# A gated recurrence of 2048 steps on one core: low fp16 parts by a scan, products in a staggered order, a hint on TensorE's outer loop

## The reference

```
z = sigmoid(y_t @ W_z + h @ U_z + vz)
r = sigmoid(y_t @ W_r + h @ U_r + vr)
hh = tanh(y_t @ W + (r * h) @ U + vh)
h = (1 - z) * h + z * hh          # out_t = y_t + h
```

## Time and profile before

| | us |
|---|---|
| median of 3 runs | 7111.71 (7102.33 to 7116.66) |
| the profiled execution | 7111.03 |
| its span, first to last instruction | 7109.2 |
| TensorE matmul busy | 6224.6 (88%) |
| VectorE busy | 5234.9 (74%), 43503 instructions |
| ScalarE busy | 3359.5 (47%) |
| mean granted TensorE clock | 0.971 |

### The profile page before, as it was taken

How to read it: one execution, slowest core, us unless ns; L and a number is a source line. 1 busy time by engine, 2 the same in 40 slices (tenths; PEclk the granted TensorE clock), 3 DMA queues, 4 the chain that set the end, 5 groups by cost and what they waited for, 6 DMA issues and landing times.

```text
span 7109.2 us, 488208 instructions
## 1 busy us (share of the span) xinstructions
PE 6224.6 (88%) x200232; PEld 5779.7 (81%) x200232; DVE 5234.9 (74%) x43503; ACT 3359.5 (47%) x22603; POOL 3.5 (0%) x13
## 2 busy tenths in 40 slices
PE   7888888888888888888888888888888888888888
PEld 7888888888888888888888888888888888888887
DVE  6777777777777777777777777777777777777777
ACT  3444444444444444444444444444444444444444
POOL 0000000000000000000000000000000000000000
PEclk8999999999999999999999999999999999999999
DMA  2000000000000000000000000000000000000000
GB/s 81 19 17 16 17 19 17 19 15 19 17 19 17 15 18 19 17 19 15 18 17 19 17 18 15 19 17 19 17 16 17 19 17 19 15 19 17 18 17 16
DMA packets 80595, 134.55 MB, mean 19 GB/s; under 512 B 12336, under 2 KB 18480, under 8 KB 80304
## 3 DMA queue, kind: packets, MB, share of 16 engines
q1 hardware_dynamic: 80304, 129.81, 5.3%
HBM read 20.46 MB, written 8.65 MB: 4 GB/s over the span
## 4 chain that ended last, share of the span: by engine, by line
PE 68%; DVE 26%; issue 5%; ACT 0%; SPq 0%; DMA 0%; ACTq 0%; DVEq 0%
PE pair_r L252 27%; PE ps_z L252 23%; PE pair_h L252 17%; DVE pair_h L481 8%; DVE h_part L528 4%; DVE h_part L518 4%; DVE h_part L537 4%; DVE keep L519 2%; DVE h_part L523 2%; DVE zn L532 2%; PE ps_p L224 0%; PE ps_z L212 0%; DMA u_raw<-in_L_cond_U 0%; DVE rh_part L490 0%; DVE ps_z L481 0%
## 5 line engine op out<-in xcount | busy, mean ns | idle before, releaser
L252 PEld LDWEIGHTS pair_r<-h_part,u_part 128*128 128x128 f16 x65536 | 1783.8, 96 | 1146.9 <-DVE h_part L537 1027.8
L252 PE MATMUL pair_r<-h_part,u_part 128*128 128x32 f16 x65536 | 1985.4, 177 | 801.9 <-DVE h_part L537 686.2
L252 PE MATMUL pair_h<-rh_part,u_part 128*128 128x32 f16 x65536 | 2120.3, 177 | 9.7 <-DVE rh_part L499 8.3
L252 PE MATMUL ps_z<-h_part,u_part 128*128 128x32 f16 x65536 | 1971.2, 177 | 45.4 <-issue 45.4
L252 PEld LDWEIGHTS pair_h<-rh_part,u_part 128*128 128x128 f16 x65536 | 1907.2, 96 | 104.4 <-DVE rh_part L499 11.6
L252 PEld LDWEIGHTS ps_z<-h_part,u_part 128*128 128x128 f16 x65536 | 1802.2, 96 | 48.0 <-issue 48.0
L481 DVE TENSOR_REDUCE pair_r<-pair_r 128x4 f32<-128x20 f32 x4096 | 742.4, 186 | 744.8 <-PE pair_r L252 723.4
L345 ACT ACTIVATE pair_r<-pair_r 128x4 f32<-128x4 f32 x4096 | 640.6, 158 | 1360.8 <-DVE pair_r L481 1291.5
L481 DVE TENSOR_REDUCE pair_h<-pair_h 128x4 f32<-128x12 f32 x4096 | 717.7, 175 | 697.7 <-PE pair_h L252 697.7
L345 ACT ACTIVATE th_z<-ps_z 128x8 f32<-128x8 f32 x2048 | 362.6, 177 | 1132.8 <-DVE ps_z L481 1132.8
L345 ACT ACTIVATE pair_h<-pair_h 128x4 f32<-128x4 f32 x4096 | 647.0, 158 | 393.4 <-DVE pair_h L481 393.0
(11 more groups left out here) (70 smaller groups left out, 3299.5 us busy)
## 6 DMA issues: line engine op xcount, KB each, us to landing
w_stage<-w_in SPq DMA_DIRECT2D x384, 256.0 KB, 2.3
x_tok<-in_x SPq DMA_DIRECT2D x68, 128.0 KB, 2.6
out_dram<-o_tok SPq DMA_DIRECT2D x66, 128.0 KB, 2.4
mlp_w<-in_L_cond_W SPq DMA_DIRECT2D x2, 1024.0 KB, 6.8
u_raw<-in_L_cond_U_r SPq DMA_DIRECT2D x1, 1024.0 KB, 5.6
u_raw<-in_L_cond_U_z SPq DMA_DIRECT2D x1, 1024.0 KB, 7.7
u_raw<-in_L_cond_U SPq DMA_DIRECT2D x1, 1024.0 KB, 10.4
w_in<-in_L_cond_W_r SPq DMA_DIRECT2D x4, 256.0 KB, 9.8
```

Of the source, the lines that this page charges most:

```text
L252: last = nc.tensor.matmul(bank[:, SLOT * m:SLOT * m + WIDE].rearrange("p (r n) -> p r n", n=n), u_part[:, g, part, k, gm * P:(gm + 1) * P] ...
```

## The change

Three things are changed.

1. Low parts. The tile `r_scan` holds for each value three columns: 0, the tanh, h_cur; `n_scan` holds 0, the tanh, z_mul. The fp16 tiles get three columns too: for the high part of r * h (-1, -1, high), of new (-1, 0, high). A scan over these triples, state = factor * state - term, gives after the third step of each value (1 + tanh) * h - high, or z_mul * tanh - high: the low part, which it writes as the third column of the low tile. So the full fp32 value of a half is no longer computed before the low part; `zn` for h_cur is computed at the end, once for both halves. ScalarE writes the tanh results to SBUF instead of PSUM and no longer waits for `zn1`. The matmuls' moving operand is now the third column of each triple.
2. Order. `staggered` writes r and h in the same order: with the first input half, both output chunks of half 0 and one of half 1 (12 matmuls); after the second wait, half 0 with the second input half (its `_mm` semaphore after 20 matmuls); then the rest of half 1. On VectorE, high(0), low(0), high(1), low(1) follow one another, and the sum of h's half 1 stands ahead of `new_high(0)`.
3. TensorE's outer loop is opened with `hint_back_edge=True`, which puts a prefetch hint for the loop's closing branch at the top of each turn.

```
-        h_cur = sb("h_cur", [P, S])
-        h_part = sb("h_part", [P, K, 2 * PARTS, B], F16)
-        rh_part = sb("rh_part", [P, K, PARTS, B], F16)
+        r_scan = sb("r_scan", [P, S, 3])
+        n_scan = sb("n_scan", [P, S, 3])
+        h_cur, z_mul = r_scan[:, :, 2], n_scan[:, :, 2]
+        h_part = sb("h_part", [P, 2 * PARTS, K, B, 3], F16)
+        rh_part = sb("rh_part", [P, PARTS, K, B, 3], F16)
...
-                moving = parts[:, k, :, :].rearrange("p a b -> p (a b)").unsqueeze(1).broadcast_to([P, WIDE // n, n])
+                moving = parts[:, :, k, :, 2].unsqueeze(1).broadcast_to([P, WIDE // n, n // B, B])
...
+            def staggered(banks, g, parts, src, name, t1):
+                def product(mh, m, kh):
+                    for k in range(kh * HC, (kh + 1) * HC):
+                        last = tile_product(banks[mh], m, g, mh * HC + m, k, parts, k == 0 and m == 0)
+                    return last
+                pe.wait_ge(s[src + "0"], t1)
+                for m in range(HC):
+                    product(0, m, 0)
+                product(1, 0, 0)
+                pe.wait_ge(s[src + "1"], t1)
+                for m in range(HC):
+                    last = product(0, m, 1)
+                last.then_inc(s[name + "0_mm"], 1)
+                for m in range(1, HC):
+                    product(1, m, 0)
+                for m in range(HC):
+                    last = product(1, m, 1)
+                last.then_inc(s[name + "1_mm"], 1)
...
-                    for kh in range(2):
-                        pe.wait_ge(s[f"hs{kh}"], t1)
-                        for mh in range(2):
-                            for m in range(HC):
-                                for k in range(kh * HC, (kh + 1) * HC):
-                                    last = tile_product(ps_r[mh], m, R, mh * HC + m, k, h_part, k == 0 and m == 0)
-                            if kh == 1:
-                                last.then_inc(s[f"r{mh}_mm"], 1)
+                    staggered(ps_r, R, h_part, "hs", "r", t1)
...
-                    for mh in range(2):
-                        for kh in range(2):
-                            if mh == 0:
-                                pe.wait_ge(s[f"rh{kh}"], t1)
...
+                    staggered(ps_h, H, rh_part, "rh", "h", t1)
...
-            with pe.Fori(0, NB) as n:
+            with nc.Fori(0, NB, engines=[mybir.EngineType.PE], hint_back_edge=True) as n:
...
-                        tanh(ps_r[hf][:, TANH:TANH + HS], ps_r[hf], R, HS, f"r{hf}_sum", t1, f"r{hf}_th")
+                        tanh(r_scan[:, half[hf], 1], ps_r[hf], R, HS, f"r{hf}_sum", t1, f"r{hf}_th")
...
-                    act.wait_ge(s["zn1"], t1)
                     seed(pair_h, H, nxt)
...
+                def low(part, hi, hf, factors, done):
+                    V.tensor_tensor_scan(triples(part[:, hi + 1, kc[hf]]), factors[:, half[hf]].rearrange("p s c -> p (s c)"),
+                                         triples(part[:, hi, kc[hf]]), 0.0, ALU.mult, ALU.subtract).then_inc(s[done], 1)
...
-                gated_high(0)
-                gated_full(0)
-                gated_high(1)
-                gated_low(0)
-                gated_full(1)
-                gated_low(1)
+                for hf in range(2):
+                    gated_high(hf)
+                    gated_low(hf)
...
                 def new_low(hf):
-                    dve.wait_ge(s[f"zn{hf}"], t1)
-                    V.tensor_tensor(h_part[:, kc[hf], NEW + 1, :], kb(zn[:, half[hf]]), h_part[:, kc[hf], NEW, :],
-                                    ALU.subtract).then_inc(s[f"hs{hf}"], 1)
-
-                new_high(0)
+                    dve.wait_ge(s[f"nhi{hf}"], t1)
+                    low(h_part, NEW, hf, n_scan, f"hs{hf}")
+
                 dve.wait_ge(s["h1_mm"], t1)
                 total(ps_h[1], H, HC, "h1_sum")
-                new_full(0)
+                new_high(0)
                 keep_low()
                 new_low(0)
                 new_high(1)
-                new_full(1)
                 new_low(1)
-                V.tensor_tensor(h_cur[:, :], keep[:, :], zn[:, :], ALU.add).then_inc(s["h_ok"], 1)
+                V.tensor_tensor(zn[:, :], z_mul, n_scan[:, :, 1], ALU.mult).then_inc(s["zn_ok"], 1)
+                dve.wait_ge(s["zn_ok"], t1)
+                V.tensor_tensor(h_cur, keep[:, :], zn[:, :], ALU.add).then_inc(s["h_ok"], 1)
```

More of the change, by code:

```diff
@@ L92, in gru_kernel @@
         keep = sb("keep", [P, S])
-        z_mul = sb("z_mul", [P, S])
         zn = sb("zn", [P, S])
@@ L113, in gru_kernel @@
                  "seed0 h0_ready r0_mm r1_mm z_mm z_keep h_ok h0_mm h1_mm r0_sum r1_sum z_sum h0_sum h1_sum r0_th r1_th z_th h0_th h1_th "
-                 "rh32_0 rh32_1 rh0 rh1 keep_ok zn0 zn1 hs0 hs1 copied")
+                 "rhi0 rhi1 rh0 rh1 keep_ok nhi0 nhi1 hs0 hs1 zn_ok copied scan_zero")
         s = {n: ctx.enter_context(nc.semaphore("s_" + n)) for n in names.split()}
@@ L249, in tile_product @@
                 n = (ADDENDS[g] - 1) * B
-                moving = parts[:, k, :, :].rearrange("p a b -> p (a b)").unsqueeze(1).broadcast_to([P, WIDE // n, n])
+                moving = parts[:, :, k, :, 2].unsqueeze(1).broadcast_to([P, WIDE // n, n // B, B])
                 for part in range(PARTS):
-                    last = nc.tensor.matmul(bank[:, SLOT * m:SLOT * m + WIDE].rearrange("p (r n) -> p r n", n=n),
+                    last = nc.tensor.matmul(bank[:, SLOT * m:SLOT * m + WIDE].rearrange("p (r a b) -> p r a b", a=n // B, b=B),
                                             u_part[:, g, part, k, gm * P:(gm + 1) * P], moving,
@@ L362, in steps @@
                     A(z_keep[:, :], th_z[:, :], ACT.Copy, scale=-0.5, bias=0.5).then_inc(s["z_keep"], 1)
-                    A(z_mul[:, :], th_z[:, :], ACT.Copy, scale=H_SCALE / 2, bias=H_SCALE / 2)
-                    tanh(ps_h[0][:, TANH:TANH + HS], ps_h[0], H, HS, "h0_sum", t1, "h0_th")
+                    A(z_mul, th_z[:, :], ACT.Copy, scale=H_SCALE / 2, bias=H_SCALE / 2)
+                    tanh(n_scan[:, half[0], 1], ps_h[0], H, HS, "h0_sum", t1, "h0_th")
                     seed(ps_z, Z, nxt)
-                    tanh(ps_h[1][:, TANH:TANH + HS], ps_h[1], H, HS, "h1_sum", t1, "h1_th")
-                    act.wait_ge(s["zn1"], t1)
+                    tanh(n_scan[:, half[1], 1], ps_h[1], H, HS, "h1_sum", t1, "h1_th")
                     seed(pair_h, H, nxt)
@@ L384, in _ @@
             act.wait_ge(s["h_ok"], T)
-            A(hist[:, (T - 1) % (2 * TB), :], h_cur[:, :], ACT.Copy).then_inc(s["copied"], 1)
+            A(hist[:, (T - 1) % (2 * TB), :], h_cur, ACT.Copy).then_inc(s["copied"], 1)
             put_out(NB + 1)
@@ L482, in total, with triples @@
                                        cols(bank, g, 0, m).rearrange("p m a b -> p m b a"), AX_X, ALU.add).then_inc(s[done], 1)
+            def triples(a):
+                return a.rearrange("p k b c -> p (k b c)")
             def step(t1):
                 kc = (slice(0, HC), slice(HC, K))
+                def low(part, hi, hf, factors, done):
+                    V.tensor_tensor_scan(triples(part[:, hi + 1, kc[hf]]), factors[:, half[hf]].rearrange("p s c -> p (s c)"),
+                                         triples(part[:, hi, kc[hf]]), 0.0, ALU.mult, ALU.subtract).then_inc(s[done], 1)
                 def gated_high(hf):
                     dve.wait_ge(s[f"r{hf}_th"], t1)
[L490 to L495, removed]
+                    V.scalar_tensor_tensor(rh_part[:, 0, kc[hf], :, 2], kb(r_scan[:, half[hf], 1]), 1.0,
+                                           kb(h_cur[:, half[hf]]), ALU.add, ALU.mult).then_inc(s[f"rhi{hf}"], 1)
                 def gated_low(hf):
-                    dve.wait_ge(s[f"rh32_{hf}"], t1)
-                    V.tensor_tensor(rh_part[:, kc[hf], 1, :], kb(rh[:, half[hf]]), rh_part[:, kc[hf], 0, :],
-                                    ALU.subtract).then_inc(s[f"rh{hf}"], 1)
+                    dve.wait_ge(s[f"rhi{hf}"], t1)
+                    low(rh_part, 0, hf, r_scan, f"rh{hf}")
                 for hf in range(2):
@@ L517, in step @@
                 dve.wait_ge(s["z_keep"], t1)
[L518 to L519 removed]
+                V.tensor_tensor(h_part[:, KEEP, :, :, 2], kb(z_keep[:, :]), kb(h_cur), ALU.mult)
+                V.tensor_tensor(keep[:, :], z_keep[:, :], h_cur, ALU.mult).then_inc(s["keep_ok"], 1)
                 def keep_low():
                     dve.wait_ge(s["keep_ok"], t1)
[L523 removed]
+                    V.tensor_tensor(h_part[:, KEEP + 1, :, :, 2], kb(keep[:, :]), h_part[:, KEEP, :, :, 2], ALU.subtract)
                 def new_high(hf):
                     dve.wait_ge(s[f"h{hf}_th"], t1)
[L528 to L533 removed]
+                    V.tensor_tensor(h_part[:, NEW, kc[hf], :, 2], kb(z_mul[:, half[hf]]),
+                                    kb(n_scan[:, half[hf], 1]), ALU.mult).then_inc(s[f"nhi{hf}"], 1)
                 def new_low(hf):
[L536 to L540 removed]
```

(3 more changed lines are left out.)

25 lines of the change are left out of this document (9 added, 16 removed).

## The result

| | before | changed |
|---|---|---|
| median, us | 7112.88 (7102.33 to 7116.66, 4 runs) | 8899.45 (8873.95 to 8921.37, 4 runs) |
| span of the profiled execution | 7109.2 | 8918.2 |
| mean granted TensorE clock | 0.971 | 0.514 |
| VectorE busy, instructions | 5234.9, 43503 | 5228.9, 37359 |

The changed kernel takes 1.2513 times as long as the one before, with a 95% interval of 1.2467 to 1.256. The forecast was 6715 us, 0.944 times. The page of the changed kernel has the granted clock, the instruction queue and the chain that ended last as follows; they answer to the earlier trace rows.

A forecast was written before the change was run, and what follows sets the result against it. One loop-carried chain through TensorE and VectorE was taken as the bound. 7111 less 287 (shorter step) less 113 (hint) is 6711, put at 6715 us for turns that gain less; own range 6640 to 6775, 8-in-10 range 6620 to 6940.

The forecast's parts named there:

- The moving operand: TensorE's matmuls read at a stride of three fp16 values: no cost taken; reading at half pace would cost 0.13 us a step.
- rival 1: Reads of k = 2 straddle 16-byte lines: 1.6 ns more for a quarter of the matmuls, 6785 us; chance 0.10.
- Rival 4: Strided read sets TensorE's pace, three columns' time spent for each: 40 ns a matmul, 9190 us; chance 0.08.
- The scan and the tail: On VectorE a scan takes 0.18 us; `new_high(0)` to `new_low(0)` falls from 0.34 to 0.195, gain 0.145.
- The stagger: TensorE's r and h order: both 0.07 us waits inside the step go; h's half 0 costs 0.10 on the chain.
- The hint: At TensorE's outer-loop turns the 3.15 us stop goes, 98 us, and 15 us of the second pause; together 113 us.
- a pause of about 1.0 stays: Second pause at an outer-loop turn, in TensorE's first step: about 1.0 us where 1.37 was; 15 us taken as gained.
- nine instruction blocks as before: Sign in the instruction queue: each outer-loop turn still fetches nine blocks, 288 in all before the change.

## Why the prediction was wrong

**The step that failed is "The moving operand"**: "I take nothing, the lower bound, and keep 0.13 and worse as rivals". The measured price is 0.97 us a step, 1994 of the 2184 us between forecast and measurement. The strided read alone in the kernel before gives 1.2576, the contiguous read in the changed kernel 0.973. The bound of 0.13 was wrong because I took the low clock's pace, 0.87 for 32 matmuls, for that of a read at half pace, and this for the worst of the likely cases. Chunk 2 is read at 60 / 32 = 1.9 ns a column, two and a quarter times the low clock's pace, at either clock.

The mechanism was named in rival 1, with its place (chunk 2, bytes 28 and 34) and the page of the Trainium skill that describes it (SBUF — State Buffer, the note on cachelines in the section Door 1: The DMA port swizzle); only its price, 1.6 ns a matmul, was an estimate from the wrong row. It is 34 ns for each of those matmuls and 6 for the other ones of r and z. The Trainium skill's rule, 16-byte lines that want two hits each, agrees with the 60 ns that moved with the straddling pair and left with it (of the width of a line the runs rule out 8 bytes, but not 32). It doesn't explain that r and z stay at 31 ns with two hits a line. An estimate from the rows comes nearer: a straddling operand changes its line at each of 32 columns, 60 / 32 = 1.9 ns a change, and one with two values a line at 16, which makes 30. But h changes its line 16 times too, between two lines and not four, and stays at 25; no run here settles why. Rival 4 had the size by luck: 40 ns a matmul against 38 measured on the average, 9190 us against 8899. Its mechanism, the time of three columns for each one read, would have made all chunks alike. Its chance of 0.08 was too small for an operand whose only evidence was cover that no row had tested.

**The clock**, of which the forecast said nothing for the changed kernel, fell to 0.514. It did not follow the pace of the matmuls alone: the means are 0.97 in the kernel before and 0.94, 0.912 and 0.909 in three others whose 32 matmuls of 32 columns take 0.82 us (contiguous read, the same in the old order, stagger alone), 0.907 where z takes 0.97, 0.51 at 1.22, and 0.50 with 8 or 16 columns. What lowers it stays open. It costs little by itself, 106 us where the columns were cut to 8 in the kernel before.

**The scan and the tail** were right: 183 ns, 0.19 from high to scan, a step of 3.21 to 3.23 against 3.205. Three things are missing in the 190 us between 6715 and the 6905 with contiguous reads. The store of the projection (90 us) was not in the sum, though h_cur moved back and r's sums forward. The wait for hs1 is 0.04, where I had 0.01, and the ordinary step 0.03 longer (57 us for 2048). And the step after the one without a projection takes 3.38, some 0.14 more, 54 us for 384 of them. The packed trace shows what stands in it: VectorE turns its inner loop there (branch at 3008.04, register work until 3008.47), between h_cur and r's first sum, which comes 0.93 after the step's start instead of 0.74; with the store left out it is the same 0.94. In the kernel before, whose h_cur is earlier, the sum comes at 0.80 in this step as in the others. No run takes the branch away. The 19 us that the hint gave beyond the forecast go against these: 90 + 57 + 54 - 19 = 182 of the 190.

**The stagger** was right in sum, as the ordinary step shows, but I had booked it in two places as if its gain were its own. By itself it loses 260 us; it gains only together with the scan.

**The hint** gained 132 us against 113. The step "a pause of about 1.0 stays" was wrong: both pauses went. So was the sign "nine instruction blocks as before": there are 8 or 9 in all instead of 288.

## What to carry to other kernels

When an edit changes how TensorE's moving operand lies in SBUF, look first at where the bytes of neighbouring columns lie against 16-byte boundaries; a layout made for one engine's instruction (here the scan's triples) is paid by every matmul that reads it. That a matmul takes some nanoseconds longer than its columns need is no bound for a read that no row shows: test it alone first. And when a chain is shortened, work that was hidden behind its slack, as the fifth step's store, has to be counted again.

## What the runs showed of the hardware

- A matmul of 32 fp16 moving columns, eight or four values repeated, at clock 1.00: 25 ns contiguous. As pairs in four places 48 or 64 bytes apart, the two of a pair 6 or 8 bytes apart and in one 16-byte line, 30 to 31; in two such places 25. With the pair on two sides of a boundary 60. With 8 columns all take 26 to 28 at clock 0.50.
- The slow reads take the same time at granted clock 0.50 and 1.00 (z 1.227 us at both).
- A scan of 12 elements takes 183 ns and one of 16 takes 192.
- The hint at the outer loop's top left 8 instruction fetches in all, where there were nine at each of 32 turns, 288 of 16.4 KB each, and took away the pauses of up to 3.9 us at the turns.
